# A graph layer of 104 blocks: narrower one-hot, row-tiled repeat, component sums on VectorE, new order of the small work

## The reference, cut to what matters

```python
r = edge_vec / norm(edge_vec); sh1 = SQRT3 * r
s1 = concat(x[src][:, :8], x[dst][:, :8])            # scalars
v1 = concat(x[src][:, 8:], x[dst][:, 8:])            # 16 vectors of 3
vdot1 = einsum('euk,ek->eu', v1, sh1) / SQRT3        # sum over the 3 components
w  = mlp(emb, fc1_w1, fc1_w2);  s_t, v_t = mix(s1, v1, vdot1, sh1, w)
w2 = mlp(emb, fc2_w1, fc2_w2);  scal, gates, vecs = mix(s_t, v_t, sh1, w2)
edge_out = concat(tanh(scal), vecs * tanh(gates)) * norm
out = layernorm(x + segment_sum(edge_out, dst))
```

## Time and profile before

| | |
|---|---|
| median of 3 runs | 809.54 us (808.5 to 809.83) |
| the profiled execution | 807.87 us, of which span 806.0 us |
| VectorE busy | 739.8 us, 92% |
| TensorE matmuls busy | 707.5 us, 88% |
| GpSimd busy | 626.8 us, 78% |
| ScalarE busy | 551.1 us, 68% |
| mean granted TensorE clock | 0.993 |

### The profile page before, as it was taken

The page is one execution under the profiler, slowest core; times in us unless marked ns, Lnnn a source line. Parts: engine busy times, 40 slices in busy tenths (PEclk is TensorE's granted clock), DMA queues, the critical chain, the costliest instruction groups (busy, mean ns, idle before and its releaser), DMA issues.

```text
span 806.0 us, 19013 instructions
## 1 busy us (share of the span) xinstructions
PE 707.5 (88%) x5819; PEld 292.3 (36%) x5922; DVE 739.8 (92%) x1217; ACT 551.1 (68%) x1279; POOL 626.8 (78%) x863
## 2 busy tenths in 40 slices
PE   1687999999999999999999999899999998999974
PEld 1432333333333333333333333333333333333322
DVE  8689999999999999999999999999999999999884
ACT  2367667777777777777776777777777767777642
POOL 8788888788888888888888888888888888888300
PEclk9899999999999999999999999999999999999998
DMA  3321211111111111211112111111111111111000
GB/s 102 89 65 19 44 26 37 24 42 27 38 26 41 24 26 39 43 24 25 36 25 44 26 38 23 42 27 37 27 41 23 26 34 36 26 23 26 12 1 20
DMA packets 44030, 27.24 MB, mean 34 GB/s; under 512 B 22012, under 2 KB 42509, under 8 KB 43930
## 3 DMA queue, kind: packets, MB, share of 16 engines
q1 hardware_dynamic: 29681, 18.24, 8.5%
q0 software_dynamic: 13312, 6.84, 5.7%
q10 hardware_dynamic: 937, 0.93, 0.4%
HBM read 21.77 MB, written 4.20 MB: 32 GB/s over the span
## 4 chain that ended last, share of the span: by engine, by line
DVE 31%; issue 29%; PE 26%; ACT 10%; DVEq 3%; ACTq 0%; POOL 0%; POOLq 0%
PE ps L917 12%; DVE z_s L714 11%; PE ps L879 7%; DVE p_s L686 6%; ACT v_s L488 5%; PE ps L857 3%; ACT ohs L483 3%; DVEq L692 3%; DVE acc L697 2%; DVE m L724 2%; PE ps L831 2%; DVE oh L588 2%; DVE m L729 2%; ACT fe L469 2%; DVE gsc L734 2%
## 5 line engine op out<-in xcount | busy, mean ns | idle before, releaser
L337 POOL DMA_INDIRECT xs<-in_xp,src_i x416 | 435.6, 1047 | 110.1 <-issue 79.3
L686 DVE TENSOR_TENSOR p_s<-ps,h 128x2048 f32<-128x2048 f32 x104 | 238.2, 2291 | 41.0 <-PE ps L917 36.3
L714 DVE TENSOR_TENSOR z_s<-ps,h 128x2048 f32<-128x2048 f32 x104 | 237.8, 2286 | 2.5 <-PE ps L879 2.3
L488 ACT CAST v_s<-ps 128x512 bf16<-128x512 f32 x312 | 181.9, 583 | 48.4 <-PE ps L857 39.1
L451 ACT COPY oht<-ps 126x512 bf16<-126x512 bf16 x104 | 61.0, 586 | 115.8 <-PE ps L831 110.6
L917 PE MATMUL ps<-f,w_f 32*128 32x512 f32 x832 | 119.6, 641 | 17.1 <-DVE z_s L714 7.5
L850 PE MATMUL ps<-p_s,sum_m 128*32 128x512 f32 x832 | 110.8, 604 | 4.9 <-DVE m L731 3.6
L879 PE MATMUL ps<-v_s,rep_m 128*128 128x512 bf16 x315 | 85.3, 379 | 26.4 <-DVE acc L697 22.7
L863 PE MATMUL ps<-z_s,w_z 128*32 128x512 f32 x832 | 108.1, 591 | 0.0
L463 ACT COPY u<-ps 128x512 f32<-128x512 f32 x104 | 61.1, 588 | 56.7 <-PE ps L863 56.7
L857 PE MATMUL ps<-v_s,less 128*128 128x512 bf16 x206 | 80.3, 390 | 13.6 <-ACT v_s L488 3.6
(11 more groups left out here) (116 smaller groups left out, 904.8 us busy)
## 6 DMA issues: line engine op xcount, KB each, us to landing
emb<-e_dram SPq DMA_DIRECT2D x312, 30.0 KB
xs<-in_xp,src_i POOLq DMA_INDIRECT x416
e_dram<-e_part SPq DMA_DIRECT2D x7, 360.0 KB
e_in<-in_emb SPq DMA_DIRECT2D x8, 240.0 KB
window<-x_dram SPq DMA_DIRECT2D x104, 7.9 KB
x_dram<-eo_all SPq DMA_DIRECT2D x3, 195.3 KB
eo_all<-in_vec_t SPq DMA_DIRECT2D x1, 528.0 KB, 4.1
xt_n<-in_xt SPq DMA_DIRECT2D x1, 400.0 KB, 3.7
```

The source lines that it names most:

```text
L337: nc.gpsimd.indirect_dma_start(xs_r[n][:, t, :], None, xp, bass.IndirectOffsetOnAxis(src_i[:, m * T + t:m * T + t + 1], axis=0)).then_inc( ...
L488: nc.scalar.copy(v_s[:], v_ps).then_inc(v_step, 1)
L686: nc.vector.tensor_tensor(p_s[:], ps[:, 0:4, :], h1_r[m % 2][:].unsqueeze(1).to_broadcast([128, 4, BE]), ALU.mult).then_inc(p_done, 1)
L714: nc.vector.tensor_tensor(z_s[:], ps[:, 0:4, :], h2_r[k % 3][:].unsqueeze(1).to_broadcast([128, 4, BE]), ALU.mult).then_inc(z_done, 1)
```

## The change

The one-hot becomes 42 wide, and the three parts of x lie side by side in a window row, so that `rows` is three accumulating matmuls per tile instead of one. `repeat` uses, for group g, only the 32 rows of that group. GpSimd no longer sums `along`; VectorE does with one reduction, `sum_along`. `gates` is split: m1, m4 and m5 stay ahead of `products2`, while m2 and gsc (`gate_sums`) go behind it. `outputs` and `over_nodes` come one and two steps later, and the loop has two more steps. TensorE's and ScalarE's calls within a step are put in another order, one half of `hidden` (`hidden_2`) goes to the end of TensorE's step. At the start the first one-hots come ahead of most constants, some constants are made in step 0, x is stored in one transfer instead of three, and ScalarE issues the first load of `emb`. At the end the last `turn` writes bank 0, and there are more `keep_warm`.

```diff
-        x_dram = nc.dram_tensor("x_dram", (PARTS, N + WIN, D), BF16, kind="Internal").ap()
+        x_dram = nc.dram_tensor("x_dram", (N + WIN, PARTS * D), BF16, kind="Internal").ap()
-        window_r = [sb(f"window{n}", [WK, D], BF16) for n in range(3)]
-        oh_r = [sb(f"oh{n}", [128, T, WK], BF16) for n in range(OH)]
+        window_r = [sb(f"window{n}", [WIN, PARTS, D], BF16) for n in range(3)]
+        oh_r = [sb(f"oh{n}", [128, T, WIN], BF16) for n in range(OH)]
...
                 nc.gpsimd.tensor_tensor(fe[:, :, 1:4, 16:32], fe[:, :, 0:1, 0:16].to_broadcast([128, T, 3, 16]), r,
                                         ALU.mult).then_inc(directed, 1)
-                pool.wait_ge(fe_step, 2 * m + 1)
-                nc.gpsimd.tensor_tensor(pair[:], along[:, :, 0, :], along[:, :, 1, :], ALU.add).then_inc(fe_step, 1)
-                pool.wait_ge(fe_step, 2 * m + 2)
-                nc.gpsimd.tensor_tensor(fe[:, :, 0, 16:32], pair[:], along[:, :, 2, :], ALU.add).then_inc(along_done, 1)
...
+            def sum_along(m):
+
+                dve.wait_ge(directed, m + 1)
+                nc.vector.tensor_reduce(fe_r[m % 2][:, :, 0, 16:32], along_r[m % 2][:].rearrange("p t k u -> p t u k"), AX.X, ALU.add
+                                        ).then_inc(along_done, 1)
...
             for i in STEPS:
-                if i == NB + 3:
+                if i == NB + 4:
                     flag = dve.value_load(misfits[0:1, 0:1], min_val=0, max_val=EP)
                 if real(i):
                     products(i)
-                if real(i - 4):
-                    accumulate(i - 4)
                 if real(i - 3):
                     gates(i - 3)
                 if real(i - 1):
                     products2(i - 1)
+                if real(i - 5):
+                    base = base_of(i - 5)
+                if real(i - 4):
+                    gated(i - 4)
+                if real(i - 5):
+                    accumulate(i - 5, base)
                 if real(i - 3):
-                    outputs(i - 3)
-                if real(i + 5) and i + 5 >= 2:
+                    gate_sums(i - 3)
+                if real(i - 4):
+                    outputs(i - 4)
+                if real(i + 2):
+                    sum_along(i + 2)
+                if real(i + 5) and i + 5 >= 4:
                     one_hot(i + 5)
+                if i == 0:
+                    late_constants()
...
-                    last = nc.tensor.matmul(ps[:, g, :], rep_m[:, g].rearrange("p j c -> p (j c)"), v_s[:],
+                    last = nc.tensor.matmul(ps[:, g, :], rep_m[32 * g:32 * g + 32, g].rearrange("p j c -> p (j c)"), v_s[32 * g:32 * g + 32],
                                             start=True, stop=True)
...
                 for t in range(T):
-                    last = nc.tensor.matmul(rows_ps[:, t, :], oht_r[m % 2][:, TE * t:TE * t + TE], window_r[m % 3][:],
-                                            start=True, stop=True)
+                    for n in range(PARTS):
+                        last = nc.tensor.matmul(rows_ps[:, t, :], oht_r[m % 2][:, TE * t:TE * t + TE],
+                                                window_r[m % 3][:, n, :], start=(n == 0), stop=(n == PARTS - 1))
```

ScalarE's step, with `copy_oht` and `tanhs` moved behind the second `part_of_v`:

```diff
             for i in STEPS:
-                if real(i + 4):
-                    copy_oht(i + 4)
-                if real(i - 3):
-                    copy_one_hot(i - 3)
...
                 if real(i):
                     part_of_v(i, 1)
-                if real(i + 1):
-                    hidden_2(i + 1)
...
                 if real(i + 3):
                     copy_rows(i + 3)
+                if real(i + 3) and i >= 2:
+                    copy_sources(i + 3)
+                if real(i + 4) and i + 4 >= 1:
+                    copy_oht(i + 4)
                 if real(i):
                     part_of_v(i, 2)
+                if real(i - 3):
+                    tanhs(i - 3)
```

More of the change, by code:

```diff
@@ L24 @@
 PARTS = 3
-WK = PARTS * WIN
 OH = 10
@@ L113, in program @@
         m4 = sb("m4", [128, T, 3, 8])
-        m5 = sb("m5", [128, T, 3, 8])
+        m5_r = [sb(f"m5_{n}", [128, T, 3, 8]) for n in range(2)]
         ohs_r = [sb(f"ohs{n}", [128, T, WIN]) for n in range(2)]
@@ L697, in accumulate, with gated @@
                 nc.vector.tensor_tensor(nodes, nodes, node_ps, ALU.add).then_inc(acc_done, 1)
-            def outputs(k):
+            def gated(k):
                 gates = eo_all[:, k, :, 0:16]
@@ L927, in keep_warm @@
                 for _ in range(n):
[L928 removed]
+                    nc.tensor.matmul(ps[:, 1, 0:128], ident[:], ident[:], start=True, stop=True)
             def nodes_themselves():
@@ L939, in _ @@
                     repeat(i - 1)
-                if real(i + 4):
-                    turn_one_hot(i + 4)
+                if real(i):
+                    sum_1(i)
+                if real(i - 5):
+                    over_nodes(i - 5)
+                if real(i + 3):
+                    rows(i + 3)
                 if i == -4:
@@ L944, in _ @@
                     keep_warm(8)
-                if real(i):
-                    sum_1(i)
-                if real(i + 3):
-                    rows(i + 3)
                 if i == -3:
@@ L960, in _ @@
                     first_layer(i + 1)
+                if real(i + 4):
+                    turn_one_hot(i + 4)
                 if real(i):
                     less_part(i, 1)
-                if real(i - 3):
-                    over_nodes(i - 3)
                 if real(i - 1):
                     sum_2(i - 1)
+                if real(i - 2):
+                    turn(i - 2)
                 if real(i + 2):
                     turn_features(i + 2)
-                if real(i - 2):
-                    turn(i - 2)
+                if real(i + 1):
+                    hidden_2(i + 1)
                 if i == NB:
```

162 lines of the change are left out of this document (91 added, 71 removed).

## The result

The changed kernel took **784.86 us** (median of 4 runs, 783.91 to 787.0) against 809.23 of the kernel before beside it (808.5 to 809.83): ratio 0.9703, interval 0.9679 to 0.9726. The prediction was 782, range 760 to 807. The profiled execution has a span of 783.4 us. In five groups of runs the kernel before had a median of 809 to 811 us, in four others (e1 to e4, f2 and f5, g1, h2) one of 964 to 973, and every time is held only against the kernel before of its own group.

The account below looks back on a forecast made before the run. The prediction took the ring of PSUM banks 0 to 3 (7.07 us) as the bound, then TensorE's row (6.85). Span: 806.0 - 21.6 - 1.8 - 3 + 1 = 780.6; forecast 782 us, range 760 to 807.

Parts of the forecast that it names:

- ring of banks: PSUM banks 0 to 3, through `products`, `repeat`, `products2` and `first_layer`: said to set the old step of 7.07 us.
- can be there after 2.99: VectorE's way from `products` to `products2`: 2.99 us instead of 3.43, with fewer small instructions between.
- The tiled repeat: Four matmuls on 32 rows each: 0.45 us instead of 1.04, bounds 0.39 and 1.04.
- factor of 3.07: The Trainium skill's speedup for four row tiles, cited as also putting the four `repeat` matmuls at about 0.45 us.
- TensorE's step, the bound: TensorE's row, 3.90 us from `first_layer` to `repeat` and 2.94 back: 6.84, taken as 6.85, bounds 6.77 and 6.97.
- VectorE's need: VectorE's own work per step in the changed kernel: 6.60 us, hardly changed from 6.57.
- rival of VectorE's floor: TensorE's blocks pack closer, so VectorE's 6.60 us per step binds: 757 us, chance 0.2.
- Twelve matmuls of rows: Between `sum_1` and `less_part` on TensorE: 0.33 us, up 0.22, hidden in a wait with 0.3 of cover.
- GpSimd against VectorE: Rival: L379, from 6.35 us after `products`, meets `one_hot`; 806 us if every step, 793 if every other; chance 0.2.
- Start: Before the first `products`: 3 us sooner through an earlier `first_layer`, bounds 0 and -5.
- Single longer steps: Time lost in the loop's single longer steps: 9 us kept of the 10.8 us before.
- End: Behind the last `products`: +1 us, from shorter `repeat`, later `over_nodes` and more `keep_warm`; bounds -1 and +3.

Follow-up runs that it names:

- e1: The kernel before with only the row-tiled `repeat`: 966.17 us against 973.25, ratio 0.974.
- e4: The changed kernel with the sum over the three components back on GpSimd as two adds: 1027.54 us against 973.25, ratio 1.0502.
- f2: The kernel before with only the row-tiled `repeat`: 937.78 us against 969.67.
- f5: The changed kernel with `hidden_2` ahead beside the first half and the sums over nodes in bank 4: 1043.83 us against 969.67, ratio 1.1036.
- g1: The changed kernel with `hidden_2` ahead, x stored in four transfers and eight `keep_warm` matmuls fewer: 1043.63 us against 971.03.
- h2: The kernel before with only the row-tiled `repeat`: 971.19 us against 964.07.
- h1: The changed kernel with the untiled `repeat` over all 128 rows: 835.39 us against 810.72, ratio 1.0308.
- h3: The kernel before with only the row-tiled `repeat`: 809.15 us against 810.43, ratio 0.9986.
- f1: The changed kernel with the second half of hidden 64 columns wide instead of 512 after the first block: 771.93 us against 808.91, ratio 0.9535.
- h4: The changed kernel with `hidden_2` ahead, x stored in four transfers and eight `keep_warm` matmuls fewer: 808.89 us against 810.68, ratio 0.9974.

## Why the prediction was right, and where not

**The ring before, and why it opens.** The ring of banks with its 7.07 was right. But it was not the only ring of that length. The prediction put the 0.09 that m1 waits for `turn` down as slack of VectorE and never summed the way on which it lies: `first_layer` to `turn` 2.96 (408.16 to 411.12), to m1 0.64 (404.69, one step of 7.07 later), to `products2` 1.03, to `first_layer` 2.44, in all 7.07. h1 and h3 show it from both sides: everything but the tiled `repeat` gives +24.7 us, the tiled `repeat` alone -1.3, both -24.4. The prediction had the two parts, that VectorE "can be there after 2.99" and that `repeat` falls to 0.50, but didn't say that each without the other is worth nothing. The new order of TensorE's work belongs to it too, since `turn` now comes 2.73 after `first_layer` (382.78 to 385.51), and fewer gates stand behind it.

**The tiled repeat.** 0.45 was taken, 0.40 measured (the view of L912: 416 matmuls of 384 to 385 ns, four of them in 0.40). That is 2.6 times as fast as the 1.03 of h1. The 0.45 that the prediction ascribes to the factor of 3.07 doesn't follow from it: 1.04 / 3.07 is 0.34, below one lone matmul of 0.39.

**TensorE's step, the bound.** Right: 6.84 summed, 6.85 taken, 6.85 measured. The parts erred by little and against each other: the row to `repeat` 3.97 instead of 3.90, in which the going over to 32-row tiles (h1) is 0.09 and the rest came out 0.02 shorter, the way back 2.88 instead of 2.94. f1 shows that this row was the bound.

**VectorE's need.** 6.60 was the sum, and 6.60 to 6.62 is the length of the steps of the changed kernel and of f1 in which VectorE waits for nothing. `one_hot` 0.32 and `sum_along` 0.36 were forecast as 0.33 and 0.35. The rival of VectorE's floor (757) falls by f1, and with TensorE's row shortened there the ring through `turn` still held the step at 6.66.

**Twelve matmuls of rows.** 0.39 from the start of L925 (388.31) to the start of L944 (388.70), where 0.33 was the sum; hidden, as said: `first_layer` waits 0.54 behind them.

**GpSimd against VectorE.** The place was right, 0.05 to 0.1 decided who waits. L377 was due at 6.35 after `products` and came at 6.67; `one_hot` was ahead of it, and GpSimd waited. In h1, where it came ahead by 0.05, VectorE lost 0.3, so this rival was a real one. The Trainium skill, "SBUF — State Buffer", Who interferes with whom, says that a VectorE instruction with two SBUF inputs contends with a GpSimd instruction that reads SBUF, and that the order of issue decides who blocks. The traces agree, with both orders on record: `one_hot` at 0.65 for 0.32, and L377 at 0.60 for 0.53.

**Start: the step that failed.** Forecast -3, bounds 0 and -5; measured +3.0 (38.2 for 35.2), outside the bounds. I followed TensorE's chain and took the loads as they were. The store of x in one transfer, a line of the change, was the late one: issued at 14.90, and the windows could be loaded at 24.24, against 18.49 before. It and `keep_warm` behind the first `rows`, with its 3.78, lie on the chain that ended last. That merging the store made it late is not shown by itself. ScalarE's store of the first 360 KB of edge attributes, issued at 20.37 before, is now issued at 15.03 beside it, in h4 too, and from 16 to 18 the transfer engines are 79% busy where they were 19%; no run parted the two.

**Single longer steps.** I kept 9 us; 709.1 - 103 x 6.85 = 3.5 were lost. VectorE's 0.2 of slack per step lets it catch up: a step with GpSimd's long split beside `outputs` takes 7.15 (L710 0.67 instead of 0.21) and the next 6.61. f1, without that slack, loses 0.10 a step.

**End.** Forecast +1, bounds -1 and +3; measured +3.3, outside the bounds. `nodes_themselves`, which took 2.89 instead of 1.55, is 1.3 of it; what the rest is, no run shows.

So the time was right to 3 us by some luck: three errors, +6 at the start, -5.5 in the longer steps and +2.3 at the end, nearly cancelled around a loop step that was right.

## What to carry to other kernels

When a ring of waits is summed, look for a second way through it that is equally long, and follow each engine's "own" work back to what its first instruction waits for (here m1 for `turn`). A faster instruction gives nothing until the way beside it is made shorter too, and each half alone can even cost (here +24.7 and -1.3, together -24.4). Before an instruction is moved, list who reads and who writes its buffer in the same step, since the new wait may lie on an engine that the edit doesn't mention (h4, 42 us). Merging transfers that had been issued as their parts came ready makes all readers wait for the last part; what this costs was not measured by itself here.
